# Edge loop with directly compared turned one-hots, gathers that add in memory, a second layer split throughout, and experts chosen in steps

## The reference

```python
xn = layernorm(x)
# messages: one for each edge
m = silu(concat(xn[ei], xn[ej], d2) @ mW1 + mb1)
m = silu(layer_norm(m, ln_g, ln_b) @ mW2 + mb2)
agg = segment_sum(m, ei)
x = x + xn + silu(concat(xn, agg) @ uW1 + ub1) @ uW2 + ub2 + linear_attention(xn)
# experts
z = layernorm(x) * gamma + beta
top2 = top_k(z @ Wr + br, 2);  w = softmax(top2.values)
x = x + sum_over_top2(w_e * (gelu(z @ W1[e] + b1[e]) @ W2[e] + b2[e]))
```

## Time and profile before

| | |
|---|---|
| median of 3 runs | 1616.28 us (1616.26 to 1617.42) |
| the profiled execution | 1614.69 us, span 1612.9 us |
| granted TensorE clock, mean | 0.933 |
| PE busy | 1431.6 us (89%) |
| DVE busy | 1186.1 us (74%) |
| ACT busy | 981.2 us (61%) |
| POOL busy | 839.8 us (52%) |
| chain that ended last | PE 78%, DVE 13%, ACT 4%, issue 3%, DMA 2% |

### The profile page before, as it was taken

How to read it: one execution, slowest core, us unless ns; L and a number is a source line. 1 busy time by engine, 2 the same in 40 slices (tenths; PEclk the granted TensorE clock), 3 DMA queues, 4 the chain that set the end, 5 groups by cost and what they waited for, 6 DMA issues and landing times.

```text
span 1612.9 us, 34882 instructions
## 1 busy us (share of the span) xinstructions
PE 1431.6 (89%) x8790; PEld 1183.5 (73%) x8791; DVE 1186.1 (74%) x4460; ACT 981.2 (61%) x2146; POOL 839.8 (52%) x1203
## 2 busy tenths in 40 slices
PE   4565999979899999999999999999998945999991
PEld 2454665556799999999999999998996633777771
DVE  7999436652899999989999999989993466444442
ACT  1342224431688888888888888888884252666560
POOL 1487750014366666666666666666640002666651
PEclk7655999989799999999999999999999977999996
DMA  7400120001122222222222222222733062444437
GB/s 193 90 4 5 46 59 1 1 23 56 40 75 73 74 73 72 73 73 74 72 72 72 74 73 73 74 72 72 73 66 138 1 230 83 66 68 65 71 56 255
DMA packets 63010, 118.03 MB, mean 73 GB/s; under 512 B 21729, under 2 KB 41473, under 8 KB 62450
## 3 DMA queue, kind: packets, MB, share of 16 engines
q0 software_dynamic: 36560, 77.33, 20.7%
q1 hardware_dynamic: 25616, 36.80, 7.2%
q10 hardware_dynamic: 780, 3.24, 0.5%
HBM read 92.57 MB, written 24.72 MB: 73 GB/s over the span
## 4 chain that ended last, share of the span: by engine, by line
PE 78%; DVE 13%; ACT 4%; issue 3%; DMA 2%; DVEq 0%; ACTq 0%; POOLq 0%
PE ps L937 13%; PE ps L692 9%; PE ps L1029 6%; PE ps L917 6%; PE ps L907 5%; PE ps L824 5%; PE ps L904 4%; PE ps L899 4%; PE ps L900 4%; PE ps L788 3%; DVE place_val_t L1392 3%; PE ps L927 2%; DVE lane_hot_e_t L1387 2%; PE ps L1056 2%; PE ps L1055 2%
## 5 line engine op out<-in xcount | busy, mean ns | idle before, releaser
L640 POOL DMA_INDIRECT msg_t<-dst_table,stage_idx x448 | 446.9, 998 | 107.6 <-issue 46.3
L937 PE MATMUL ps<-msg_t,hot_t 128*125 128x256 f32 x896 | 241.5, 392 | 13.7 <-issue 7.4
L1160 ACT ACTIVATE msg1n_t<-msg_t,nw_b,nw_y 128x256 f32<-128x256 f32 x448 | 243.7, 598 | 0.0
L1177 ACT ACTIVATE msg_t<-msg_t 128x512 f32<-128x512 f32 x224 | 141.5, 632 | 100.9 <-DVE msg_t L1572 100.8
L899 PE MATMUL ps<-w_hi_t,msg1T_hi_t 128*128 128x256 f32 x672 | 198.5, 310 | 0.0
L606 POOL DMA_INDIRECT sorted_edges<-sort_sb_t,chunk_to x112 | 136.0, 1214 | 86.2 <-DVE chunk_to L1379 52.7
L900 PE MATMUL ps<-w_lo_t,msg1T_hi_t 128*128 128x256 f32 x672 | 179.8, 282 | 0.0
L937 PEld LDWEIGHTS ps<-msg_t,hot_t 128*125 128x125 f32 x896 | 151.2, 188 | 31.8 <-issue 9.6
L917 PE MATMUL ps<-src_hi_t,hotT_t 127*128 x448 | 160.8, 379 | 3.7 <-ACT hotT_t L1173 3.7
L1572 DVE TENSOR_TENSOR msg_t<-ps,msg_t 128x512 f32<-128x512 f32 x224 | 152.5, 681 | 3.4 <-PE ps L917 3.4
L904 PE MATMUL ps<-w_hi_t,msg1T_lo_t 128*128 128x256 f32 x672 | 153.6, 283 | 0.0
(11 more groups left out here) (346 smaller groups left out, 3569.5 us busy)
## 6 DMA issues: line engine op xcount, KB each, us to landing
w_sb_t<-in_L_ffn_W_dram SPq DMA_DIRECT2D x16, 512.0 KB, 7.9
msg_t<-dst_table,stage_idx POOLq DMA_INDIRECT x448, 2.8
res_t<-in_x_dram SPq DMA_DIRECT2D x1, 3125.0 KB
total<-zero_chunks_t SPq DMA_DIRECT2D x1, 3125.0 KB, 39.4
dst_table<-dst_stage SPq DMA_DIRECT2D x25, 125.0 KB
xm_table<-xm_t POOLq DMA_DIRECT2D x5, 625.0 KB, 7.4
total<-res_t SPq DMA_DIRECT2D x1, 3125.0 KB
sum_b_t<-total ACTq DMA_DIRECT2D x5, 625.0 KB, 11.2
```

Source lines behind the costliest of these rows:

```text
L640: pool.indirect_dma_start(out=msg1[:, k, j, :], out_offset=None, in_=dst_table, in_offset=bass.IndirectOffsetOnAxis(stage_idx[:, half, q:q ...
L937: m = pe.matmul(bank(7, D, rows=NP), hot[:, (k - 8) % TURN, j, 0:NP].bitcast(F32), msg2[:, k % 2, j, :], start=(j == 0), stop=(j == G - 1))
L1160: m = A(msg1n[:, (k + 1) % 2, j, :], msg1[:, kk, j, :], ACT.Identity, bias=nw_b[:, kk, j:j + 1], scale=nw_y[:, kk, j:j + 1])
L1177: A(v, v, ACT.Silu).then_inc(msg1_sb, 1)
```

## The change

- **Turned one-hots.** The row numbers of all edges are written to HBM once (`row_list`, half precision). In the loop SP reads those of five units back, broadcast over all partitions (`near_rows`), and VectorE compares them with each partition's own number: `hotT` directly, ten units deep. The `d2` parts go through HBM too, into rows 126 and 127 of `hotT`. The transposing product, its copy, and `edge_weights` go. `hot` (edges in partitions, for the sum) is compared as before, later in the step, and two units deep.
- **Gathers that add.** ScalarE copies the source part from PSUM to `msg1`; then GpSimd's gathers add `dst_table`'s rows onto it in memory (`compute_op=ALU.add`). VectorE's add goes. A gather now waits for `pre_sb` of its own unit. The SiLU and all later stages come three steps later (`LAG = 3`).
- **Second layer.** All four parts are computed in three products of reduced precision.
- **Block numbers** are read one by one.
- **Choice of experts in steps.** Raw logits are copied block by block, the inverse root is a power on GpSimd by chunk, `max` and `max_index` and the normalized copies `xm` follow by chunk within the update. Counts are summed over a row first, so that the two products have 8 columns each instead of 400. TensorE waits for `w2_rest` only before the first product that reads it. The store of `res` to HBM is issued in two parts, of 112 and 13 partitions.

```diff
+    LAG = 3
+    NEAR = 5
-        recs = at("recs_t", [128, TILES, 4], F32, "edges")
+        recs = at("recs_t", [128, TILES, 2], F32, "edges")
+        near_rows = [at(f"near_rows{h}", [128, NEAR, UE], F16, owner, byte)
+                     for h, (owner, byte) in enumerate((("weights", 5632), ("edges", TILES * 8)))]
-        hot = at("hot_t", [128, TURN, G, 128], F32R, "weights", filled["weights"])
+        hotT = at("hotT_t", [128, TURN, UE], F32R, "weights", filled["weights"])
...
# SP
+            sp.wait_ge(side_out, 48)
+            sp.wait_ge(w2_split, 1)
+            for h, m in enumerate(range(0, UNITS, NEAR)):
+                some = min(NEAR, UNITS - m)
+                if h >= 2:
+                    sp.wait_ge(hotT_sb, m - NEAR)
+                sp.dma_start(near_rows[h % 2][:, 0:some, :].rearrange("p k e -> p (k e)"),
+                             row_list[m * UE:(m + some) * UE].partition_broadcast(128)).then_inc(near_in[h % 2], 16)
+                if h >= 2:
+                    sp.wait_ge(pre_ps, m - NEAR)
+                sp.dma_start(hotT[NP:HR, m % TURN:m % TURN + some, :].bitcast(F32),
+                             weight_rows[:, m * UE:(m + some) * UE].rearrange("v (k e) -> v k e", e=UE))\
+                  .then_inc(weights_in[h % 2], 16)
...
# GpSimd
-                    after(pool, msg1n_sb, TURN * (i - 1) + k + 1)
+                    pool.wait_ge(pre_sb, TURN * i + k + 1)
                     carry_wait(k)
                     for j in range(G):
                         q = G * (k % HALF) + j
                         pool.indirect_dma_start(
                             out=msg1[:, k, j, :], out_offset=None, in_=dst_table,
-                            in_offset=bass.IndirectOffsetOnAxis(stage_idx[:, half, q:q + 1], 0))\
-                            .then_inc(row_in[k], 16)
-                    edge_weights(TURN * i + k - LATER, (k - LATER) % TURN)
+                            in_offset=bass.IndirectOffsetOnAxis(stage_idx[:, half, q:q + 1], 0),
+                            compute_op=ALU.add).then_inc(row_in[k], 16)
+            for c in range(len(CH)):
+                T = slice(CH[c][0], CH[c][-1] + 1)
+                pool.wait_ge(var2_ok, c + 1)
+                pool.tensor_tensor(rstd[0:NP, T], rstd[0:NP, T], minus_half[0:NP, 0:len(CH[c])], ALU.pow).then_inc(sd2_ok, 1)
...
# TensorE, late = n - LAG, kl = (k - LAG) % TURN
-                        if len(split) < KD:
-                            m = pe.matmul(o[j], msg1T_f[:, (k + 1) % 2, :], w2c[:, KD - 1, :], start=False, stop=True)
+                        for c in range(KD):
+                            m = pe.matmul(o[j], part(msg1T_lo, j, c), w2_hi[:, c, :], start=False, stop=(c == KD - 1))
-                    after(pe, hotT_sb, n + 1)
+                    pe.wait_ge(hotT_sb, n + 1)
+                    if k % NEAR == 0:
+                        pe.wait_ge(weights_in[k // NEAR], turn_weights)
-                    for j in range(G):
-                        m = pe.matmul(bank(0, 128, rows=HR, first=j * 128), hot[:, (k + 1) % TURN, j, 0:HR], ident_r[:],
-                                      start=True, stop=True)
-                    m.then_inc(hotT_ps, 1)
-                if k in (1, 5):
-                    load_blocks(mybir.EngineType.PE, blk, n + 2, k + 2, 4 if k == 1 else 3)
+                if k < TURN - 1:
+                    load_blocks(mybir.EngineType.PE, blk, n + 1, k + 1, 1)
-            pe.wait_ge(w2_rest_ok, NE)
+                    if isinstance(m_, int) and m_ == 0:
+                        pe.wait_ge(w2_rest_ok, NE)
...
# ScalarE
-                    A(msg1T_hi[:, k % 2], bank(3 + k % 2, SPLIT), ACT.Copy)
-                    A(msg1T_f[:, k % 2], bank(3 + k % 2, 128, first=SPLIT), ACT.Copy).then_inc(msg1T_sb, 1)
+                    A(msg1T_hi[:, kl % 2], bank(3 + kl % 2), ACT.Copy).then_inc(msg1T_sb, 1)
-                    A(hotT[0:HR, (k + 1) % 2, :], bank(0, UE, rows=HR), ACT.Copy).then_inc(hotT_sb, 1)
                 if here(n, UNITS):
-                    act.wait_ge(pre_sb, n + 1)
-                    v = msg1[:, k].rearrange("p j n -> p (j n)")
+                    act.wait_ge(pre_ps, n + 1)
+                    after(act, msg1n_sb, n - TURN + 1)
+                    A(msg1[:, k].rearrange("p j n -> p (j n)"), bank(1 + k % 2), ACT.Copy).then_inc(pre_sb, 1)
+                if here(late, UNITS):
+                    act.wait_ge(row_in[kl], turn_rows)
+                    v = msg1[:, kl].rearrange("p j n -> p (j n)")
                     A(v, v, ACT.Silu).then_inc(msg1_sb, 1)
...
# VectorE
+                    dve.tensor_scalar(hotT[0:NP, kk, :], near_rows[kk // NEAR][0:NP, kk % NEAR, :], row_col[0:NP, :], None,
+                                      ALU.is_equal).then_inc(hotT_sb, 1)
-                if here(n, UNITS):
-                    dve.wait_ge(pre_ps, n + 1)
-                    dve.wait_ge(row_in[k], turn_rows)
-                    v = msg1[:, k].rearrange("p j n -> p (j n)")
-                    dve.tensor_tensor(v, bank(1 + k % 2), v, ALU.add).then_inc(pre_sb, 1)
...
+                if c >= 2:
+                    pick(c - 2)
+                if 1 <= c < len(CH) - 1:
+                    spread_of(c - 1)
```

More of the change, by code:

```diff
@@ L330, in gps_layer @@
         wtmp = inside("wtmp", [128, NB], F32, "late")
-        nbias = inside("nbias", [128, NB], F32, "late")
+        nbias = at("nbias", [128, NB], F32, "edges", 1696)
         e_cum = inside("e_cum", [128, NE], F32, "late")
@@ L661, in _, with store_rows @@
                       allow_small_or_imprecise_dtypes=True).then_inc(token_ok, 1)
-            for g in range(5):
+            def store_rows(g):
                 pool.wait_ge(xm_ok, 5 * (g + 1))
@@ L831, in turn_records @@
             def turn_records(g):
-                for v in range(FIELDS):
+                for v in range(2):
                     m = turn(bank(RECS[g], LT, first=v * LT),
@@ L975, in route @@
                 pe.wait_ge(x2T_sb, t + 1)
+                after(pe, logit_ok, t)
                 for k in range(KD):
@@ L1003, in _ @@
             pe.wait_ge(hotk_ok, 1)
-            flat = hot_k[0:NP].rearrange("p e m -> p (e m)")
-            pe.matmul(bank(3, NE * KT, rows=NP), earlier[0:NP, 0:NP], flat, start=True, stop=True)
-            pe.matmul(bank(4, NE * KT, rows=NP), ones[0:NP, 0:NP], flat, start=True, stop=True).then_inc(route_ps, 1)
+            pe.matmul(bank(3, NE, rows=NP), earlier[0:NP, 0:NP], row_n[0:NP, :], start=True, stop=True)
+            pe.matmul(bank(3, NE, rows=NP, first=NE), ones[0:NP, 0:NP], row_n[0:NP, :], start=True, stop=True)\
+              .then_inc(route_ps, 1)
             for g in range(KT // BATCH):
@@ L1614, in add_hidden, with raw_logits, spread_of, pick @@
                 m.then_inc(hid_pre, 1)
+            def raw_logits(t):
+                if t >= 0:
+                    dve.wait_ge(logit_ps, t + 1)
+                    dve.tensor_copy(logits[R, t, :], bank(7, NE, rows=NP, first=t * NE)).then_inc(logit_ok, 1)
+            def spread_of(c):
+                T = slice(CH[c][0], CH[c][-1] + 1)
+                st.join()
+                dve.tensor_scalar(rstd[R, T], meanvar[R, T, 1], 1.0 + EPS, EPS * EPS, ALU.mult, ALU.add).then_inc(var2_ok, 1)
+            def pick(c):
+                blocks, n = CH[c], len(CH[c])
+                T = slice(blocks[0], blocks[-1] + 1)
+                dve.wait_ge(sd2_ok, c + 1)
+                dve.wait_ge(logit_ok, blocks[-1] + 1)
+                dve.scalar_tensor_tensor(nbias[R, T], meanvar[R, T, 0], -1.0, rstd[R, T], ALU.mult, ALU.mult)\
+                   .then_inc(rstd2_ok, 1)
+                step(dve.tensor_tensor(logits[R, T], logits[R, T], rstd[R, T].unsqueeze(2).broadcast_to([NP, n, NE]), ALU.mult))
+                step(dve.tensor_tensor(logits[R, T], logits[R, T], logit0[R].unsqueeze(1).broadcast_to([NP, n, NE]), ALU.add))
+                for t in blocks:
+                    st.did(dve.max(top_v[R, t, :], logits[R, t, :]))
+                st.join()
+                for t in blocks:
+                    st.did(dve.max_index(top_e[R, t, :], top_v[R, t, :], logits[R, t, :]))
             dve.wait_ge(mixed_ok, NB)
@@ L1622, in _ @@
                 for t in blocks:
+                    raw_logits(t - 3)
                     dve.wait_ge(upd_ps, t + 1)
@@ L1636, in _ @@
             st.join()
-            dve.tensor_copy(nw_t[R, 0, 0:1], meanvar[R, 0, 0:1]).then_inc(var2_ok, 1)
-            dve.wait_ge(sd2_ok, 1)
-            step(dve.reciprocal(rstd[R], rstd[R]))
-            dve.scalar_tensor_tensor(nbias[R], meanvar[R, :, 0], -1.0, rstd[R], ALU.mult, ALU.mult).then_inc(rstd2_ok, 1)
-            dve.wait_ge(logit_ps, NB)
-            step(dve.tensor_tensor(logits[R], bank(7, NB * NE, rows=NP).rearrange("p (t e) -> p t e", e=NE),
-                                   rstd[R].unsqueeze(2).broadcast_to([NP, NB, NE]), ALU.mult))
```

(12 more changed lines are left out.)

281 lines of the change are left out of this document (148 added, 133 removed).

## The result

The changed kernel takes 1690.12 us (median of 4, 1687.8 to 1691.25), the kernel before 1616.27 on the same chip: a ratio of 1.0454, 95% interval 1.0436 to 1.0472. The forecast was 1689.4. The profiled execution has a span of 1687.7, 74.8 above that of before.

A forecast was written before the change was run, and what follows sets the result against it. TensorE was taken to bound the old loop, at 3.51 us a unit, and GpSimd the new one, at 3.94. The loop's 87.1 us less 14.0 for the choice of experts gave +73.1, so 1689.4; range 1560 to 1712.

The forecast's parts named there:

- The signs: Edge loop: GpSimd busy over 85%, adding gathers at 1.55 to 1.65 us, period 3.9, TensorE busy some 83%.
- The price of a gather that adds: GpSimd's queue: 1.59 us per adding gather, taken from the adding scatter; bounds 0.97 and 1.59.
- GpSimd's unit: Edge loop: 3.82 us plus 0.05 for the cast and 0.07 for slower gathers, together 3.94 against 3.51.
- Begin and end of the loop: Edge loop: first gather at 410.1, GpSimd's units end at 1292.7, loop ends at 1315.8, 87.1 us later.
- SP's queue priced nothing: Edge loop: row broadcasts and weight rows through SP's queue, every 19 us against a landing of some 4 us, cost nothing.
- The update: Node update: the earlier picks' work lies in VectorE's waits of 5.3 us per chunk and costs nothing.
- Choice of experts: Behind the update: 9.5 us less to the list, first hidden add earlier, 14 us in all; bounds 9.5 and 16.
- Sum: Whole kernel: 87.1 - 14.0 = +73.1 us, giving 1689.4 on the median.
- The free add: Rival, edge loop: adding costs a gather nothing, TensorE bounds at 3.3 us; 1560, between 1545 and 1592; chance 0.24.
- the second rival: Edge loop: add free, but block-number reads and handoffs fill the gain; 1609, bounds 1600 to 1625; chance 0.06.
- GpSimd held up by VectorE: Rival, edge loop: VectorE's memory-to-memory compare costs each unit 0.25 us more, 56 us, 1745 in all; chance 0.08.
- The savings of the split layer and of the transposing pair: Edge loop: TensorE loses 0.17 and 0.08 us a unit, 3.51 to 3.26, hidden behind GpSimd's 3.94.

The follow-up runs named there:

- e1: The changed kernel with plain gathers that overwrite the source part instead of adding onto it; 1576.72 us, ratio 0.9765 to the kernel before.
- e2: The changed kernel with each unit's first gather adding and its second plain; 1587.99 us, ratio 0.9832 to the kernel before.
- e3: The changed kernel with the loads of the experts' first weights issued only after the last unit's SiLU is taken; 1686.28 us, ratio 1.0440.
- e4: The changed kernel with VectorE copying the waiting block's raw logits before the hidden add at each chunk's start; 1688.39 us, ratio 1.0453.
- h4: h1 with the raw logits copied ahead of the hidden add, as in e4; ratio 0.9941 to the kernel before.
- h1: The kernel before with its own edge loop, plus the changed update and stepped choice of experts; ratio 0.9964 to the kernel before.
- h2: h1 with the second layer all in three products of reduced precision; ratio 0.9988 to the kernel before.
- e5: The changed kernel with plain gathers running ahead, the add back on VectorE, ScalarE's copy gone and LAG 0; 1745.93 us, ratio 1.0325.
- g1: e5 with the compares that make hot moved from VectorE to GpSimd; ratio 1.0535 to the kernel before.

## Why the prediction was right

The mechanism was right: the add set the period, through GpSimd. The total is 0.7 us from the forecast, and that closeness is luck: the terms are off by up to 11 us, and partly cancel. The signs came with it, but for two sizes: GpSimd busy for 81% of the loop, where over 85% was named, since the gaps before the gathers don't count as busy; and TensorE 87%, where 83% was.

**The price of a gather that adds** was the step on which all hung, and held: 1.565 us on the mean for 1.592 taken from a scatter. e1 and e2 show it as the cause: the same loop without the add runs at 3.42, with one of two at 3.47, with both at 3.87. By the rule of "DMA: Bandwidth & Descriptors" in the Trainium skill, in its rules for kernel authors, that an accumulating DMA reads its destination first, the higher price was to be expected in this direction too, and the trace agrees: the DMA engines are busy for 2.13 us a unit instead of e1's 1.13. That this read is also what costs GpSimd its 0.60 us is not shown.

**GpSimd's unit** was put at 3.94 and measured 3.87: 16 us over 224 units. The unit without the cast is 3.74, not 3.82 (gathers 0.03 shorter each, the fence hidden by some hundredths); the cast costs 4.41 - 3.74 = 0.67 once in five, 0.13 a unit instead of 0.05, because the fence behind it is not hidden; and the 0.07 that gathers in a running loop were to lose did not come. In the old loop GpSimd's gathers varied more, 1.000 on the mean against 0.966; here 1.566 against 1.560.

**Begin and end of the loop.** The first gather came at 412.9, not 410.1 (whose parts add up to 410.25): 1.88 us before the first gather, for which the forecast had no term, and 0.9 in the steps ahead of it. The old trace showed such a gap of 2.07 us, and it was left out. The landing of the last took 10.9 us instead of 3.8, 7.1 more, of which e3 gave back 6.3. Together: 224 units of 3.877 from 412.90 end at 1281.3, 11.4 us under the forecast's 1292.7; the landing took 6.7 of these back (1290.15 against 1294.9), the drain behind it 1.1 (22.0 us to the last add against 20.9; in e3, whose clock did not fall there, 21.1). So the loop's end moved by 83.4 us, not 87.1. Only part of it is the period. Of the 83.4 us, 2.6 come before the first product, 13.8 from there to the first add into `agg` (40.4 for 26.6), 55.1 in the next 200 units and 12.0 in the last 24, which were quicker than the rest in the old loop (73.6 us) and less so here (85.6). "SP's queue priced nothing" was right for the broadcasts inside the loop, wrong for what the queue issues behind them: the transfers that it starts early met gathers that had become late.

**The update** was priced at nothing and costs 5.1 us (78.9 for 73.8). 3.3 of it lie in the chunks, and e4 and h4 show 2.7 of them to be the copy of the raw logits behind the hidden add. Another 0.6 of the 3.3 stays in e4. The other 1.8 lie before the last statistics, where picks of the chunks before now stand ahead of it on VectorE; that is read from the trace, no run took it away.

**Choice of experts**: 12.4 us gained for 14.0. To the list it was 7.2 instead of 9.5: the power on GpSimd takes 1.01 us by itself, where 0.9 were put for it with its handoffs, and comes twice at the end. The wait for all of w2_rest went as forecast: 37.6 us from the list's start to the first hidden add became 32.4.

**Sum**: 83.4 + 5.1 - 12.4, and 1.4 less behind the first hidden add (250.0 us for 251.4): 74.7, the difference of the spans but for rounding. The last 1.4 are not the change's doing: e3 and e4 have 251.6 and 251.5 with the same code there, by the clock shown with e3.

**The rivals.** The free add did not come, but its time can now be read: e1's 1577, inside its 1545 to 1592 and 17 above its 1560. Its period was put at 3.3 and is 3.42; the 3.51 that it was measured against was off as well, since this is the step of a unit without a stall and the old loop's mean is 3.61 (138.5 units in 500 us, in h1). What stops e1 at 3.42 is, by the chain, VectorE: its steps and its reads of block numbers (L448, 8 to 9% of the chain from 700 to 1100 us) stand on it, with 466 of 500 us busy. No run took the reads away; so the second rival, reads and handoffs that refill the gain, may have had some truth in it. At 1.27 us a gather the loop had left GpSimd (e2), which fits the threshold of 1.28 and doesn't measure it. GpSimd held up by VectorE did not come: beside a compare of two memory operands in every unit gathers took 1.566 on the mean, and the shortest 1.546. The operations beside which fetches took 1.93 are not compares, as the forecast calls them, but subtractions of 1024 columns with two memory operands (L1728), and the first fetches of the changed kernel still take 1.76 to 1.97 beside them. So such an effect exists, and the loop's shorter operations don't show it. "SBUF — State Buffer" in the Trainium skill, section "SBUF: two separate sides", has a VectorE instruction with two memory operands and a GpSimd instruction that reads SBUF exclude each other for a whole instruction; no row of the loop shows that for a gather.

**The savings of the split layer and of the transposing pair** were costed as hidden behind GpSimd, and were. h2 shows that without this cover the split alone would not have been a gain either: the 3.51 from which a gain of 18 us was expected was no period to begin with, and VectorE stood at 453 of 500.

## What to carry to other kernels

A DMA that adds is not a free add: price it on the engine that issues it (here 0.60 us more of GpSimd's time for each 128 rows, against 0.34 of VectorE's for the same rows), and compare that with the room this engine has in a unit, not with that of the engine it relieves. A transfer that must wait for work of its own unit also makes the loop's begin and end longer; against e5, which has the same period, that was some 24 us here. When a loop's last transfers become late, look at what the queues issue behind the loop. Take a period from many units and not from one step (3.61 and 3.51 here). Price a moved operation's small companions in the engine's order too: a copy of eight columns behind a 1.3 us add cost a chunk 0.7 us.

## What the runs showed of the hardware

- GpSimd's own time of an indirect DMA of 128 rows is 1.55 to 1.57 us for most gathers that add (median 1.560), 1.592 in the median for a scatter that adds, 0.966 and 0.967 for a plain gather and scatter, with 0.30 us between two of either kind. In e2 the kinds alternate and keep their times (0.99 and 1.55). Beside subtractions of 128x1024 on VectorE plain fetches took 1.75 to 1.98.
- By their busy share, a gather that adds kept the 16 DMA engines busy for about 0.5 us more than a plain one (1.13, 1.63 and 2.13 us a unit with none, one and two that add).
- A compare of 125 columns on GpSimd took 0.62 us, VectorE's of 250 elements 0.41; a power of 4 columns on GpSimd 1.01, of one column 0.58.
- Ahead of the loop's first gather stood 1.88 us without a releaser in all four runs where it adds (the changed kernel, e2, e3, e4). Where it is plain, 0.16 to 0.51 stood ahead of it and 2.07 to 2.17 ahead of the second (before, e1, e5, h1). The first fetch for the experts, behind a pause of 30.8 us, had no such gap. The cause is open.
- The granted clock fell to its lower level behind the loop's end in e2, g1, h1 and h4 and not in the others; the update's first statistics came 15.3 us behind the last add there, and 13.6 elsewhere.
